# Attention in a two-layer kernel: which queries a row-maximum tile takes, and how the maxima are read back into the score banks

## What is computed

```python
qkv = X @ W_qkv
qkv = qkv.reshape(b, s, h, d, 3)
q, k, v = (qkv[..., 0], qkv[..., 1], qkv[..., 2])
scores = jnp.einsum('bqhd,bkhd->bhqk', q, k) / scale
weights = jax.nn.softmax(scores, axis=-1)
attn = jnp.einsum('bhqk,bkhd->bqhd', weights, v)
return attn.reshape(b, s, h * d) @ W_out
```

## Time and profile before

| | before |
|---|---|
| median of three runs | 1887.1 us |
| the profiled execution, its time | 1889.88 us |
| the profiled execution, its span | 1888.0 us |
| busy of the span: PE, DVE, ACT, POOL | 95%, 80%, 78%, 77% |
| ACT seeds (L1455) | 448, 487.2 us busy |
| DVE seeds (L1681) | 64, 78.0 us busy |
| mean granted clock | 0.984 of full speed |

### The profile page before, as it was taken

The page is one execution under the profiler, slowest core; times in us unless marked ns, Lnnn a source line. Parts: engine busy times, 40 slices in busy tenths (PEclk is TensorE's granted clock), DMA queues, the critical chain, the costliest instruction groups (busy, mean ns, idle before and its releaser), DMA issues. The chain is left out here.

```text
span 1888.0 us, 32039 instructions
## 1 busy us (share of the span) xinstructions
PE 1785.0 (95%) x9247; PEld 989.1 (52%) x9247; DVE 1519.8 (80%) x2053; ACT 1464.2 (78%) x1954; POOL 1448.2 (77%) x868
## 2 busy tenths in 40 slices
PE   5799999999999999999999999999999899985687
PEld 4445444454454455554544544545445587763456
DVE  6787788888878777878878888778788788888896
ACT  4388888888888888888888888888888688874653
POOL 4288888888888888888888888888888457755564
PEclk9899999999999999999999999999999999997899
DMA  7112021212121121202121212112121577531000
GB/s 249 60 54 78 34 78 35 78 46 76 45 67 47 66 83 48 78 34 78 35 79 54 68 45 67 54 59 89 41 78 34 174 226 248 154 95 56 0 18 28
DMA packets 117014, 143.31 MB, mean 76 GB/s; under 512 B 18417, under 2 KB 98353, under 8 KB 113778
## 3 DMA queue, kind: packets, MB, share of 16 engines
q1 hardware_dynamic: 111986, 132.61, 22.4%
q0 software_dynamic: 4992, 10.27, 1.6%
HBM read 87.20 MB, written 27.64 MB: 61 GB/s over the span
## 5 line engine op out<-in xcount | busy, mean ns | idle before, releaser
L1530 POOL TENSOR_TENSOR psum_k<-psum_k,probs 128x1024 f32<-128x1024 f32 x384 | 929.9, 2422 | 144.8 <-ACT probs L1471 125.8
L1549 DVE TENSOR_REDUCE mxh<-ps_m 128x2 f32<-128x1024 f32 x518 | 623.6, 1204 | 242.7 <-PE ps_m L1285 242.6
L1471 ACT ACTIVATE probs<-ps_s 128x1024 f32<-128x1024 f32 x512 | 496.9, 1023 | 164.0 <-PE ps_s L1301 146.3
L1310 PE MATMUL ps_v<-probs,V 128*64 128x512 f32 x2056 | 494.6, 602 | 0.0
L1310 PEld LDWEIGHTS ps_v<-probs,V 128*64 128x64 f32 x2056 | 130.5, 136 | 239.2 <-issue 183.8
L1455 ACT ACTIVATE ps_s<-qkv_raw 128x1024 f32<-128x1024 f32 x224 | 243.6, 1124 | 0.0
L1455 ACT ACTIVATE ps_s<-peak 128x1024 f32<-128x1024 f32 x224 | 243.6, 1122 | 0.0
L1565 DVE RECIPROCAL e_y_row<-e_y_row 128x128 f32<-128x128 f32 x256 | 241.4, 943 | 0.0
L1530 POOL TENSOR_TENSOR psum_k<-probs 128x1024 f32<-128x1024 f32 x64 | 152.6, 2384 | 63.7 <-ACT probs L1471 47.7
L1301 PE MATMUL ps_s<-e_ew 64*128 64x512 f32 x1536 | 198.8, 390 | 0.0
L1285 PE MATMUL ps_m<-e_ew 64*128 64x512 f32 x524 | 163.9, 622 | 5.4 <-DVE mxh L1549 4.7
(11 more groups left out here) (317 smaller groups left out, 2918.0 us busy)
## 6 DMA issues: line engine op xcount, KB each, us to landing
e_ew<-w_split SPq DMA_DIRECT2D x23, 1024.0 KB
qkv_raw<-peaks SPq DMA_DIRECT2D x33, 512.0 KB, 3.9
V<-e_x_raw SPq DMA_DIRECT2D x33, 512.0 KB, 5.1
peak<-peaks SPq DMA_DIRECT2D x32, 512.0 KB, 4.1
xs_hi<-xh SPq DMA_DIRECT2D x16, 512.0 KB, 4.1
xs_lo<-xl SPq DMA_DIRECT2D x16, 512.0 KB, 5.0
rows<-in_blank_d SPq DMA_DIRECT2D x4, 1483.5 KB, 16.1
e_x_raw<-rows SPq DMA_DIRECT2D x23, 258.0 KB
```

The costliest lines, as they stand in the source:

```text
L1310: ins = nc.tensor.matmul(ps_v[rows, :], V[par][:, kt, rows], probs[:, t % RING, x, :], start=kt == 0, stop=kt == KT - 1)
L1471: nc.scalar.activation(probs[:, t % RING, :, :], ps_s[t % 2][:, :, :], ACT.Exp, scale=SCALE).then_inc(p_done, 1)
L1530: nc.gpsimd.tensor_tensor(acc, probs[:, (t - 1) % RING, :, :] if kt == 1 else acc, probs[:, t % RING, :, :], ALU.add).then_inc(add_done, 1)
L1549: nc.vector.tensor_reduce(mxh[:, kh, t, :], max_bank(unit, i)[:, :, :], AX.X, ALU.max).then_inc(m_done, 1)
```

## The change

The row-maximum tile t now takes 128 neighbouring queries, from `hf * CH + t * P` on, so its stationary operand is contiguous. Partition c then holds the maxima of queries c, 128 + c, 256 + c and 384 + c. `mx` is ordered (x, t), and is still written as one piece of 32 bytes from each partition. So `peaks` and `peak[hf]` hold the order (c, x, t): the neighbouring query of the same head is eight floats, 32 bytes, further on. The seeds of ACT and DVE read it through a view of four dimensions (p, x, t, q) and write their bank in the order of before. The two seeds before the loop (L1462) do the same.

```diff
--- before.py
+++ after.py
@@ -47,7 +47,7 @@
     g.psum_k = [sb(f"psum_k{h}", [P, 2, CH], F32) for h in range(2)]
     g.place = sb("place", [P, 2, TILES], U32)
     g.ones = sb("ones", [P, DH], F32)
-    g.mx = sb("mx", [P, 4, 2], F32)
+    g.mx = sb("mx", [P, 2, 4], F32)
     g.V = [sb(f"V{p}", [P, TPB, 2 * DH], F32) for p in range(2)]
 
     spare = g.psum_k[0][:, :, :].rearrange("p x c -> p (x c)")
@@ -1003,7 +1003,8 @@
     w_in, preset, w_staged, wlo_staged, add_done = g.attn_w_in, g.preset, g.w_staged, g.wlo_staged, g.add_done
     even = [w[:, k * T:(k + 1) * T] for w in g.w_first for k in range(2)]
     k_hi, k_lo, q_hi, q_lo = ([even[k], sb(f"{name}1", [P, T], F32R)] for k, name in enumerate(("k_hi", "k_lo", "q_hi", "q_lo")))
-    peak = [qkv[:, 2, :, :].rearrange("p a d -> p (a d)").rearrange("p (c x) -> p c x", x=2), sb("peak1", [P, CH, 2], F32)]
+    peak = [qkv[:, 2, :, :].rearrange("p a d -> p (a d)").rearrange("p (q x t) -> p x t q", x=2, t=4),
+            sb("peak1", [P, P, 2, 4], F32)[:, :, :, :].rearrange("p q x t -> p x t q")]
     V_next = g.V_next
     xs_hi = sb("xs_hi", [P, T], F32R)
     xs_lo = sb("xs_lo", [P, T], F32R)
@@ -1138,6 +1139,9 @@
     def chunk(name):
         return slice(int(name[1]) * CH, (int(name[1]) + 1) * CH)
 
+    def scores_of(tile):
+        return tile[:, :, :].rearrange("p x (t q) -> p x t q", t=4)
+
     def pairs(eng):
 
         with eng.Fori(0, N // 2) as i:
@@ -1166,9 +1170,9 @@
             def spread(unit, hf):
 
                 sp.wait_ge(mx_done, unit + 1)
-                sp.dma_start(g.peaks[hf:hf + 1, :].rearrange("a (q k) -> q (a k)", k=8), mx[:, :, :].rearrange("p t x -> p (t x)")).then_inc(mx_out, 16)
+                sp.dma_start(g.peaks[hf:hf + 1, :].rearrange("a (q k) -> q (a k)", k=8), mx[:, :, :].rearrange("p x t -> p (x t)")).then_inc(mx_out, 16)
                 sp.wait_ge(mx_out, unit * 16 + 16)
-                sp.dma_start(peak[hf][:, :, :].rearrange("p c x -> p (c x)"), g.peaks[hf:hf + 1, :].to_broadcast([P, 2 * CH])).then_inc(peak_in, 16)
+                sp.dma_start(peak[hf].rearrange("p x t q -> p (q x t)"), g.peaks[hf:hf + 1, :].to_broadcast([P, 2 * CH])).then_inc(peak_in, 16)
 
             load_part(0)
             spread(0, 0)
@@ -1280,9 +1284,9 @@
                         pe.wait_ge(m_done, unit * KT + i - 1)
                 else:
                     pe.wait_ge(m_done, unit * KT + i)
-                q = q_hi[par][:, :].rearrange("p (c t) -> p t c", t=4)[:, t, hf * P:(hf + 1) * P]
+                q = hf * CH + t * P
                 for x, rows in enumerate(HEADS):
-                    ins = nc.tensor.matmul(m[:, x, :], q[rows, :], k_hi[par][rows, kh * CH:(kh + 1) * CH],
+                    ins = nc.tensor.matmul(m[:, x, :], q_hi[par][rows, q:q + P], k_hi[par][rows, kh * CH:(kh + 1) * CH],
                                            start=True, stop=True)
                 ins.then_inc(m_ready, 1)
 
@@ -1452,14 +1456,14 @@
                 if t % KT < 2:
                     act.wait_ge(peak_in, peaks_of(n, t))
                 act.wait_ge(p_done, P0 + n * STEPS + t - 1)
-                nc.scalar.activation(ps_s[t % 2][:, :, :], peak[hf][:, :, :].rearrange("p c x -> p x c"), ACT.Copy, scale=-1.0).then_inc(seeded, 1)
+                nc.scalar.activation(scores_of(ps_s[t % 2]), peak[hf], ACT.Copy, scale=-1.0).then_inc(seeded, 1)
 
             act.wait_ge(preset, LATE_PRESETS)
             act.wait_ge(routed, 2)
             act.wait_ge(armed, 1)
             act.wait_ge(peak_in, 16)
             for k in range(2):
-                nc.scalar.activation(ps_s[k][:, :, :], peak[0][:, :, :].rearrange("p c x -> p x c"), ACT.Copy, scale=-1.0).then_inc(seeded, 1)
+                nc.scalar.activation(scores_of(ps_s[k]), peak[0], ACT.Copy, scale=-1.0).then_inc(seeded, 1)
             for n, par in pairs(act):
                 for t in range(STEPS):
                     p = t // 2
@@ -1551,7 +1555,7 @@
                     v.wait_ge(m_done, unit * KT + KT)
                     if not (isinstance(unit, int) and unit == 0):
                         v.wait_ge(mx_out, unit * 16)
-                    nc.vector.tensor_reduce(mx[:, :, :], mxh[:, :, :, :].rearrange("p k t x -> p t x k"), AX.X, ALU.max).then_inc(mx_done, 1)
+                    nc.vector.tensor_reduce(mx[:, :, :], mxh[:, :, :, :].rearrange("p k t x -> p x t k"), AX.X, ALU.max).then_inc(mx_done, 1)
 
             def low(n, name, par):
                 hi, lo = (k_hi, k_lo) if name[0] == "K" else (q_hi, q_lo)
@@ -1678,7 +1682,7 @@
 
                 v.wait_ge(p_done, P0 + n * STEPS + t - 1)
                 v.wait_ge(peak_in, peaks_of(n, t))
-                nc.vector.tensor_scalar(ps_s[t % 2][:, :, :], peak[t // KT][:, :, :].rearrange("p c x -> p x c"), -1.0, None, ALU.mult).then_inc(seeded_v, 1)
+                nc.vector.tensor_scalar(scores_of(ps_s[t % 2]), peak[t // KT], -1.0, None, ALU.mult).then_inc(seeded_v, 1)
 
             for n, par in pairs(v):
                 nxt = 1 - par
```

## The result

| | before | after |
|---|---|---|
| median | 1888.8 us (4 runs) | 2220.9 us (4 runs, 2208.4 to 2224.9) |
| ratio | | 1.174, 95% interval 1.169 to 1.180 |
| profiled execution, its time and span | 1889.88, 1888.0 | 2224.87, 2223.0 |
| one pass of the attention loop | 43.8 us, all 31 | 54.2 us on average, 52.4 to 56.0 |

What follows compares the result with a forecast made beforehand. PE bounds attention, ACT some 16% behind; longer seeds make ACT the bound. A pass goes from 43.76 to 50.7 us, 6.9 x 32 = 222 us more: 2112 for the profiled execution, 2109 against the median; range 2010 to 2200.

Steps and rivals of the forecast that it cites:

- Part 1: Row maxima's weight load on PE: contiguous operand takes 117 ns off each, at most 60 us in all, at least 0.
- the rival's figure: Gain from shorter weight loads alone if ACT's reads hide the stride: 8 x 0.2 us a pass, 51 us; chance 0.07.
- Part 2: Seeds reading peak at 32 bytes: each grows 0.84 us on ACT, to 1.96; DVE's go from 1.22 to 1.85.
- The range's upper price: Growth of a seed on ACT if the stride's price is an addition, by the weight load's row: 0.94 us, giving 2147.
- sum of waits: Attention loop: seeds, scores and exponentials added up by double step, making a pass 50.7 us against 43.76.
- DVE's longer seed still comes before its scores: DVE's two seeds a pass, done some 4.8 us after the preceding seed's end, were taken to delay nothing.
- (d): Rival: PE, no longer busy throughout, is granted 1.2 GHz in places, taking the time over 2200 us; chance 0.01.
- Part 3: Reduce of mxh into mx, SP's two transfers per unit, queues and waits: no cost; early seeds and maxima balance.
- Rival (a): ACT's seed reads hide the stride, leaving only the weight loads' gain of 51 us: 1836 us; chance 0.07.
- (b): Rival: seed reads on ACT pay half as much again, 0.43 us a seed, giving 1952 us; chance 0.06.
- (c): Rival: row maxima's weight load stays at 305 ns, moving the forecast some 25 us; chance counted inside the forecast.
- The range: 2010 to 2200 us: both ends of the price, 15 us below for smoother overlap, 50 above for hidden waits.

Runs made afterwards that it cites:

- strides: Kernel before plus quiet copies of 1024 floats after the loop, reading at steps of 4 to 128 bytes; on ACT 1.07 us at 8 bytes, 2.00 at 32.
- pe_kept_busy: Changed kernel with each even row maximum computed four times over, except at steps 2 and 14; 2188.6 us, ratio 1.154.
- dve_seeds_dense: Changed kernel with DVE's two seeds of a pass reading peak without gaps, ACT's still at 32 bytes; 2158.0 us, ratio 1.139.

## Why the prediction was wrong, by its own steps

The main mechanism was right: ACT pays for a stride of 32 bytes, becomes the bound, and PE waits for seeds. 112 us of the 332 were missing. By the passes of the profiled executions: forecast 50.7 us; with DVE's seeds dense and no dip 51.2; as it is without a dip 52.5; on average 54.2. Over 32 passes that is 16, 42 and 54 us, together 112.

- **Part 1, the weight load**: 117 ns off was said, 113 measured (305 to 192). With dense seeds a pass is 1.7 us shorter (43.8 to 42.0), seeds shorter by 0.10 us included; 1.6 was the rival's figure. Right.
- **Part 2, the price on ACT**: +0.84 us was said, from the level of 1.65 ns a float; quiet it is 0.93 from 1.07 to 2.00, in the loop 0.97, to 2.09. The range's upper price, 0.94, was just missed. On DVE 1.85 was said and 2.11 measured. The 1.65 ns came from a row at 128 bytes, and in strides 128 bytes is cheaper than 32 by 0.12 us on both engines; that would account for most of the error on ACT. The term was mis-sized by 0.13 us, which over 12 seeds and 32 passes is 50 us by the prediction's own count; as the clean pass came out at 51.2 and not 52.3, its sum of waits was too high by 1.1 us a pass, and by luck this hid most of it.
- **"DVE's longer seed still comes before its scores"**: the step that failed. It put the wait at nothing. The seed had 0.7 to 0.8 us of slack before its scores and grew by 0.9, so PE now waits for it (59 times, 33 us in the changed kernel). It also left out what stands behind the seed on DVE's own queue: the reduction of the row maximum, and behind that PE's odd row maximum and item; the slack there was 0.32 us. Both could be read in the trace of before. Together 42 us without dips.
- **(d), the clock**: given 0.01, with the reason that PE's gaps are near 1 us. The second step that failed. The gaps were as it said (no wait of PE for ACT's seeds is longer than 1.1 us), and the clock fell to 1.2 GHz for some microseconds in nearly every pass all the same, 1.7 us a pass or 54 us. pe_kept_busy got 32 us of it back, with 0.5 us of added work a pass. What set it off was not PE's idle share alone: it is 85% busy in the changed kernel from 500 to 700, at a clock of 0.96, and 84% in dve_seeds_dense, where the clock stays at 1.00. So the two unforeseen terms are not independent: with longer DVE seeds there are more dips.
- **Part 3, small things**: nothing, as said; the transfers of mx and peak land in 1.4 and some 4 us, as before.
- **Rival (a)** would have needed ACT to hide the stride: it does not. **(b)**, half a penalty, is excluded by the step in strides; POOL's own plain copy went from 1.09 to 1.99 us, 83% more. The Trainium skill (GPSIMD Engine Reference, performance pitfalls) states its 50% for custom kernels on that engine; no such kernel was run here. **(c)** is excluded by the 192 ns.
- **The range** allowed 50 us for waits counted as hidden; they and the clock were 96.

Open: what adds 0.09 us to a strided seed in the loop; how the 1.3 us a pass divides between the wait for the seed and the reduction behind it; and what makes the clock fall in one pass and not in the next. Whether pe_kept_busy with dense DVE seeds would reach the 51.2 us pass throughout was not tried.

## What to carry to other kernels

A layout change moves a stride from one reader to another; count the elements that each reads: here 128 columns a row maximum gained 0.1 us and 1024 floats a seed lost 1.0. If the reader can write in any order into PSUM, let the write take the stride and the read be dense (1.02 us a seed here, against 2.09). When an instruction grows, ask what is queued behind it on its own engine before asking who waits for its result.

## What the runs showed of the hardware

- Reads from SBUF at 4 and 8 bytes run at the engine's own speed (1.03 to 1.07 us for 1024 floats on ACT, 1.23 on DVE), from 16 bytes on at one level for all three engines, 1.87 to 2.01 us, a little cheaper at 64 and 128 bytes than at 16 and 32.
- Writes to PSUM at steps of 32 bytes, 512 bytes and 2 KB cost nothing on ACT and DVE (1.03 and 1.23 us).
- DVE's product of two SBUF operands (L1582) went from 1.24 us to 2.04 us with no change of its own. It takes 0.69 us with POOL idle. When an addition on POOL is running at its start, it ends 0.54 to 0.55 us after that addition does, in all of the 64 in the kernel before and the 63 in the changed one; so it waits for the rest of it. Two rows of the kernel before (there L1578), ending at 721.85 and 722.40:

```profile
719.46 2.39 POOL L1530 TENSOR_TENSOR psum_k<-probs 128x1024 f32<-128x1024 f32 x1 [1.23 <-ACT probs L1471]
720.76 1.64 DVE L1578 TENSOR_TENSOR e_y_row<-e_y_row 128x512 f32<-128x512 f32 x1
```

- 1152 matmuls added to PE's gaps made the kernel 32 us faster, the mean granted clock going from 0.952 to 0.984.
- A write to DRAM of 1024 pieces of 4 bytes from 128 partitions kept the read behind it waiting for 10.0 us on average, up to 11.6; as 128 pieces of 32 bytes it lands in 1.4 us.
